# Grouped-query attention: GpSimd takes a fifth key tile in every fourth unit, and keys and an output half stand at other slots

## What is computed

```python
q = (query @ Wq + bq).reshape(B, L, NKV, G, HDIM)
k_, v_ = jnp.split(kv @ Wkv + bkv, 2, axis=-1)
...
scores = jnp.einsum('blkgd,bmkd->bkglm', q, k) * scale
attn = jax.nn.softmax(scores, axis=-1)
o = jnp.einsum('bkglm,bmkd->blkgd', attn, v).reshape(B, L, NHEAD * HDIM)
return o @ Wo + bo
...
x = x + jnp.tanh(g_xattn[0]) * _L0_xattn_ref(_layernorm(x, axis=-1), ctx_4096, ...)
x = x + jnp.tanh(g_ffn[0]) * _L0_ffn_ref(_layernorm(x, axis=-1), ...)
```

## Time and profile before

| | us |
|---|---|
| time, median of 3 runs | 2287.54 (2286.14 to 2289.63) |
| the profiled execution | 2287.23 |
| its span, first to last instruction | 2285.1 |
| TensorE busy | 2239.8 |
| VectorE busy | 1858.9 |
| ScalarE busy | 1667.6 |
| GpSimd busy | 1625.9 |

### The profile page before, as it was taken

How to read it: one execution, slowest core, us unless ns; L and a number is a source line. 1 busy time by engine, 2 the same in 40 slices (tenths; PEclk the granted TensorE clock), 3 DMA queues, 4 the chain that set the end, 5 groups by cost and what they waited for, 6 DMA issues and landing times.

```text
span 2285.1 us, 37480 instructions
## 1 busy us (share of the span) xinstructions
PE 2239.8 (98%) x12299; PEld 1929.9 (84%) x12299; DVE 1858.9 (81%) x3263; ACT 1667.6 (73%) x3184; POOL 1625.9 (71%) x1373
## 2 busy tenths in 40 slices
PE   7999999999999999999999999999999999999999
PEld 6888888888888888888888888888888888888875
DVE  5898888888888787887888788787787888788786
ACT  4777777777777777777777777777777777777773
POOL 5887887977658678757658778766757657667672
PEclk9999999999999999999999999999999999999999
DMA  7444343454233343326213333333423213223120
GB/s 262 142 151 140 127 156 129 159 193 164 93 112 113 110 157 94 129 88 206 93 54 135 113 132 121 113 128 110 169 88 100 93 63 108 68 91 100 56 102 37
DMA packets 140031, 273.97 MB, mean 120 GB/s; under 512 B 22048, under 2 KB 57408, under 8 KB 139584
## 3 DMA queue, kind: packets, MB, share of 16 engines
q1 hardware_dynamic: 124864, 257.85, 33.2%
q10 hardware_dynamic: 14976, 13.74, 2.6%
HBM read 202.44 MB, written 66.97 MB: 118 GB/s over the span
## 4 chain that ended last, share of the span: by engine, by line
PE 74%; DVE 14%; issue 5%; ACT 3%; POOL 3%; DMA 1%; ACTq 0%; DVEq 0%; SPq 0%; POOLq 0%
PE psW L454 11%; PE psW L456 11%; PE psW L455 11%; PE psS L454 6%; PE psS L456 6%; PE psS L455 6%; PE psW L684 6%; PE psW L687 5%; PE psW L686 5%; DVE psum_ L1442 4%; DVE mrun L1407 3%; PE psW L511 2%; DVE pl L1160 2%; POOL xs L898 1%; PE psW L519 1%
## 5 line engine op out<-in xcount | busy, mean ns | idle before, releaser
L898 POOL TENSOR_TENSOR xs<-xs,mb 128x512 f32<-128x512 f32 x832 | 1064.6, 1303 | 458.2 <-ACT mb L969 458.2
L1407 DVE TENSOR_TENSOR mrun<-psS,mrun 128x512 f32<-128x512 f32 (+1 forms) x704 | 481.6, 684 | 281.1 <-ACT xs L969 277.8
L969 ACT ACTIVATE xs<-psS 128x512 f32<-128x512 f32 x832 | 496.9, 597 | 224.6 <-PE psS L456 213.5
L1160 DVE TENSOR_TENSOR pl<-psP,ph 128x512 fp32r<-128x512 f32 (+1 forms) x672 | 458.6, 683 | 78.7 <-ACT ph L1102 74.7
L1102 ACT ACTIVATE ph<-xs 128x512 fp32r<-128x512 f32 x832 | 520.0, 625 | 3.0 <-PE psW L687 2.7
L1442 DVE TENSOR_TENSOR psum_<-psP,psum_ 128x512 f32<-128x512 f32 (+1 forms) x672 | 457.1, 680 | 2.0
L1099 ACT ACTIVATE psP<-xs 128x512 f32<-128x512 f32 (+1 forms) x672 | 402.4, 599 | 30.3 <-POOL xs L898 12.6
L454 PE MATMUL psS<-ql,kh 128*128 128x512 f32 x832 | 341.6, 411 | 7.1 <-DVE mrun L1407 6.1
L684 PE MATMUL psW<-ph,vh 128*128 128x512 f32 x832 | 334.9, 402 | 3.8 <-DVE pl L1160 1.6
L455 PE MATMUL psS<-qh,kh 128*128 128x512 f32 x832 | 327.5, 394 | 0.0
L456 PE MATMUL psS<-qh,kl 128*128 128x512 f32 x832 | 326.7, 393 | 0.0
(11 more groups left out here) (225 smaller groups left out, 4432.2 us busy)
## 6 DMA issues: line engine op xcount, KB each, us to landing
wqh<-scr_wq SPq DMA_DIRECT2D x96, 256.0 KB, 2.6
wql<-scr_wq SPq DMA_DIRECT2D x96, 256.0 KB, 3.0
woh<-scr_wo SPq DMA_DIRECT2D x47, 512.0 KB, 3.3
wol<-scr_wo SPq DMA_DIRECT2D x47, 512.0 KB, 4.2
rbc<-scr_r ACTq DMA_DIRECT2D x52, 256.0 KB, 3.4
scr_wq<-wqh SPq DMA_DIRECT2D x32, 256.0 KB, 2.2
scr_wq<-wql SPq DMA_DIRECT2D x32, 256.0 KB, 2.9
scr_wo<-woh SPq DMA_DIRECT2D x16, 512.0 KB, 2.7
```

The costliest lines, as they stand in the source:

```text
L898: eng.tensor_tensor(tile, tile, mb[:, U % 2, :], ALU.subtract).then_inc(s_sub)
L969: return eng.activation(hi, src, ACT.Copy)
L1160: return eng.tensor_tensor(lo, src, f32(hi), ALU.subtract)
L1407: eng.tensor_tensor(run, psS[0:rows, s % 2, :], a, ALU.max).then_inc(s_m)
```

## The change

Two things, in batches 1 to 3 the first, in all batches the second.

First, a function `by_pool(U)` says which tiles of a unit are GpSimd's. It is as before, save that in batches 1 to 3 units with U % 4 == 1 give it tile 4, the fifth, too. There are twelve (17, 21, ... 61); since tiles are worked on one unit later, the work lies in units 18, 22, ... 62, the third units of four. GpSimd makes the tile's lower part (L4) and adds the tile to the pair (A4); VectorE leaves both out. The full exponential of that tile goes to a third place of `pp`. The counts that the engines wait for (`ap_tile`, `ap_total`) follow.

Second, the last unit but one of a batch (14, 30, 46, 62) gets a string of its own: output half p0 stands in slot 1 instead of 4, the keys' last chunk k3 in slot 4 instead of 6.

```diff
--- before.py
+++ after.py
...
         return 1 if U < NU else 3
+    def by_pool(U):
+        return (0,) if U < NU else (0, 1, 2, 4) if U % 4 == 1 else (0, 1, 2)
     MEM_LO, MEM_SUM = 2, UN - 3
...
     ]
+    LAST_BUT_ONE = "m,v11 p0 b,v12 k2 k3 s - r,p1 q0 - q1 x0 o0,x1"
     TURN = "m,v11 p0 b,v12 k2 p1 s k3 r q0 - q1 - o0"
...
                     UN + 1: "- p1 c - s - o0 o1",
-                    UN - 1: "m - b - p1 s - r - - o0 - -"}.get(U, TURN if U > NU and U % NU == 2 else (AT_MEM if U >= MEM_LO + 2 else AT)[U % 4])
+                    UN - 1: "m - b - p1 s - r - - o0 - -"}.get(U, TURN if U > NU and U % NU == 2 else LAST_BUT_ONE if U % NU == NU - 2 else (AT_MEM if U >= MEM_LO + 2 else AT)[U % 4])
         for t, names in enumerate(names_of.split()):
...
         mrun = sb("mrun", [128, 2, 512], F32)
-        pp = sb("pp", [128, 2, 512], F32)
+        pp = sb("pp", [128, 3, 512], F32)
         mb = sb("mb", [128, 2, 512], F32)
...
             U, t = divmod(T, NT)
-            pool_tile = t < lead(U)
+            pool_tile = t in by_pool(U)
             for c, more in ((l_count, not pool_tile), (lp_count, pool_tile), (a_count, not pool_tile)):
...
                 in_psum.append(T)
+        ap_tile, ap_total, n = {}, {}, 0
+        for U in range(NU, UN):
+            if U > NU:
+                n += 1
+                ap_total[U - 1] = n
+            for a in by_pool(U)[2:]:
+                n += 1
+                ap_tile[U, a] = n
         def pair_of(U):
...
                 return psum_[:, U % 2, :]
-            if t < lead(U):
-                return pair_of(U)[:, t - 1, :]
+            if t in by_pool(U):
+                return pair_of(U)[:, by_pool(U).index(t) - 1, :]
             return psP[0:rows_of(t), (l_count[T] - 1) % 2, :]
...
                     else:
-                        pe.wait_ge(s_ap, 2 * (n - NU + 1))
+                        pe.wait_ge(s_ap, ap_total[n])
                     turn(("s", n, 0), psum_[:, n % 2, :], s_su, s_r, n + 1, sum_by_mem(n))
...
                     pe.wait_ge(s_vl, NT * (U // 4) + v_made(t))
-                    if t < lead(U):
+                    if t in by_pool(U):
                         pe.wait_ge(s_lp, lp_count[T])
...
             def add_p(T):
+                U, t = divmod(T, NT)
                 pool.wait_ge(s_lp, lp_count[T])
-                pair = pair_of(T // NT)
-                eng.tensor_tensor(pair[:, 0, :], pair[:, 0, :], pair[:, 1, :], ALU.add).then_inc(s_ap)
+                if t == 4:
+                    pool.wait_ge(s_ap, ap_tile[U, 2])
+                pair = pair_of(U)
+                eng.tensor_tensor(pair[:, 0, :], pair[:, 0, :], pair[:, by_pool(U).index(t) - 1, :], ALU.add).then_inc(s_ap)
             def merge(U):
...
                 pool.wait_ge(s_a, a_count[NT * U + NT - 1])
-                pool.wait_ge(s_ap, 2 * (U - NU) + 1)
+                pool.wait_ge(s_ap, ap_tile[U, by_pool(U)[-1]])
                 eng.tensor_tensor(total, pp[:, 0, :], total, ALU.add).then_inc(s_ap)
...
                 "S0,S1 M,S2 L0,S3 L1,S4 L2,S5 A2,S6 S7 S8 S9 S10 S11 S12 -",
-                "S0,S1 S2,S3 S4,L0 L1,L2 M,S5 S6,A2 S7 S8 S9 S10 S11 S12 -")]
+                "S0,S1 S2,S3 S4,L0 L1,L2 M,S5 S6,A2 S7 S8 S9 S10 S11 S12 -",
+                "S0,S1 M,S2 L0,S3 L1,S4 L2,S5 A2,S6 L4,S7 A4,S8 S9 S10 S11 S12 -")]
             for p in first:
...
                 if 0 <= U < UN:
-                    for step in steps_at[0 if lead(U) == 1 else 2 if U == UN - 1 else 1][t]:
+                    for step in steps_at[0 if lead(U) == 1 else 3 if 4 in by_pool(U) else 2 if U == UN - 1 else 1][t]:
                         if step == "M" and U > 0 and lead(U - 1) == 3:
...
                             act.wait_ge(s_su, U - 1)
-                    elif t < lead(U):
+                    elif t in by_pool(U):
                         if U == UN - 1:
...
                         elif U > NU:
-                            act.wait_ge(s_ap, 2 * (U - NU))
+                            act.wait_ge(s_ap, ap_total[U - 1])
                         else:
...
                 T = s - EXP
-                if 0 <= T < TN and T % NT >= lead(T // NT):
+                if 0 <= T < TN and T % NT not in by_pool(T // NT):
                     UT, tt = divmod(T, NT)
...
                         dve.wait_ge(s_a, a_count[T])
-                        dve.wait_ge(s_ap, 2 * (UT - NU) + 1)
+                        dve.wait_ge(s_ap, ap_tile[UT, 2])
                         eng.tensor_tensor(total, pair_of(UT)[:, 0, :], total, ALU.add).then_inc(s_a)
...
```

## The result

The changed kernel takes 2291.18 us (median of 14 runs, 2289.56 to 2294.8), the kernel before 2286.72 beside it (14 runs, 2284.76 to 2289.63): a ratio of 1.002, 95% interval 1.0014 to 1.0027, so 0.2% slower, about 4.5. The forecast was +1.4. The profiled execution took 2291.5 (2287.23 before), with a span of 2289.5 (2285.1) and a mean granted TensorE clock of 0.996 (0.999).

The account below looks back on a forecast made before the run. TensorE, busy 98% of the span, was taken to bound the kernel, so only its waits could shrink. Terms -3.2 - 0.2 + 6.2 - 1.4 = +1.4 on 2287.23 gave 2288.6, or 2288.9 as median; 8-in-10 range 2283.3 to 2292.8.

Parts of the forecast that it names:

- Part 1: Fifth tile on GpSimd, units 22, 26, 38, 42, 54, 58: scores wait less for running max, 0.53 each, -3.2.
- Units 18, 34 and 50: Fifth tile on GpSimd there: its work stays hidden with 0.1 to spare, nothing gained, 0.
- The slower rival: Fifth tile comes late at slot 10's product in every third unit; one more operation's lag gives 2297.5; chance 0.12.
- the third rival: VectorE's stalls vanish whole (6 x 0.78, unit 62 whole, unit 14 gains 1.2): 2285.4; chance 0.10.
- Unit 14: Keys and output half sooner, but the reciprocals' spread then waits for VectorE: -0.2, bounds -1.2 and +0.3.
- Units 30 and 46: GpSimd's fifth tile behind two normalisations: TensorE stands 4.2, unit 3.1 longer (bounds +2.4, +3.6), +6.2 for two.
- The faster rival: Normalisations don't hold the product in units 30 and 46, which gain 1.1 each: 2280.3; chance 0.12.
- Unit 62: Gains 1.1 in slot 7 and 1.2 from the fifth tile; slower second normalisation costs 0.9: -1.4, bounds -2.5, -0.7.
- The signs named in the prediction: Running-max waits 0.1 to 0.2, pl wait about 4 at slot 10 of units 30 and 46 alone, kl wait gone.
- part 2: Keys and an output half sooner in units 14, 30, 46, 62; 1.1 of unit 30's 1.33 wait gained.

Follow-up runs that it names:

- E2: Changed kernel without the fifth tile on GpSimd in any unit, only keys and output half moved sooner: 2282.78, ratio 0.9982 to the kernel before.
- E7: E4 with output half p1 also one slot sooner, in slot 6 of units 14, 30, 46 and 62: 2279.39, ratio 0.9968.
- E5: Changed kernel with 17 extra matmuls, unused in the result, filling TensorE's wait in slot 10 of units 30 and 46: 2288.3, ratio 1.0004.
- E4: Changed kernel with x normalisations of units 30 and 46 moved to slot 1, x loads to slot 6 of units 29 and 45: 2281.1, ratio 0.9976.
- E1: Changed kernel, but VectorE keeps the fifth tile in units 30 and 46: 2279.71, ratio 0.9969 to the kernel before.
- E6: Changed kernel with the second of two x normalisations moved behind GpSimd's fifth-tile lower half in units 30 and 46: 2286.64, ratio 0.9993.
- E8: E1 with output half p1 also in slot 6 of units 14, 30, 46 and 62: 2279.1, ratio 0.9964 to the kernel before.
- E3: Changed kernel with only the fifth tile on GpSimd, keys and output half standing as before: 2285.41, ratio 0.9996.
- E9: E7 with the loads of x issued in slot 10 of units 29 and 45 instead of slot 6: 2280.21, ratio 0.9966.

## Why the prediction was right or wrong

**Sign and size.** Forecast +1.4 with "no difference" as likeliest; measured +4.5, which lies at the bound of 0.2%, inside the range. The miss of 3.1 is nearly all in one term.

**Part 1, six units: right.** -3.2 forecast, -3.40 measured, -0.49 to -0.63 a unit. The scores of slot 12 start within 0.01 of the forecast time, because the price was read from ScalarE's chain (0.53) and not from VectorE's saving (1.20). E2, without part 1, has +0.12 there, so the gain is part 1's.

**Units 18, 34 and 50: right.** 0 forecast, +0.11 for the three, and a margin of 0.1 was enough: the product is at 667.68 in unit 18, with no wait. The slower rival, a fifth tile late in every third unit, doesn't occur. Nor does the third rival, by which VectorE's stalls vanish whole: it wanted 0.78 from each of the six units, and 0.49 to 0.63 came.

**Unit 14: right.** -0.2 forecast, -0.31 measured. As worked out, the spread of the reciprocals waits for VectorE, and takes most of the 1.1 back. TensorE in unit 14:

```profile
522.52 0.65 PE L536 MATMUL psW<-ident,rinv 128*128 128x128 f32 x4 [1.04 <-DVE rinv L1361]
522.93 0.48 PE L471 MATMUL psW<-wol,oh 128*128 128x512 f32 x1
```

E7, which puts work in front of this wait, gets 0.7 of it back in unit 14 and loses 0.2 to 0.3 in unit 15.

**Units 30 and 46: the mechanism right, the term mis-sized.** This is the step that failed. The prediction had GpSimd's chain at 7.50, 4.11 and 1.29; measured are 7.54 (1067.04 to 1074.58), 4.10 and 1.27. It had a stand of 4.2 and a unit 3.1 longer; E5 measures 3.14 and 3.09 for exactly that stand. What it left out is what TensorE does behind a stand. The term was +6.2 for the two units; it measured +9.69, and 3.5 of that is the work at half clock. The prediction counted a pause as lost time alone and took every matmul behind it at its old duration. Its own upper bound of +3.6 a unit was worked out from GpSimd's durations only, so neither +5.30 nor +4.39 lies within it.

In these units the kernel before could not show this: they hold no idle time over 1.1. Its start-up does. TensorE of the kernel before, timeline at the end of an idle time there, and the window behind it:

```profile
30.02 0.44 PE L454 MATMUL psW<-cl,wkh 128*128 128x384 f32 x1 [3.18 <-DVE cl L1160]
```

```profile
31.20:34.50 3.30, 3.30 (x11) 3.01 (x10) 0.48 (x1) 1.17 (x2) 0.20 (x1) 0.50 0.95 310
```

This pair was the row to ask for a price: an idle time of 3.18 with the clock at half for 3.41 behind it, that is some 1.7 of work lost, beside a forecast stand of 4.2 in each unit. With it the term would have been +3.1 + 1.7 twice, +9.6, against +9.69 measured. That this agrees so well is luck: the clock cost 2.2 in one unit and 1.3 in the other, because it stayed low for 5.1 and 3.0 behind the two products (1080.01 to 1085.07, 1631.62 to 1634.61), and how long that is the kernel before could not tell.

**The faster rival** (the normalisations don't hold the product) fell; E4 and E1 show that its price was right: with the hold taken away the units are 0.9 to 1.2 shorter (it said 1.1), and the whole is at 2281.1 and 2279.71 (it said 2280.3).

**Unit 62: right by half of its reason.** -1.4 forecast, -1.37 measured. VectorE in unit 62, the place of the earlier trace rows:

```profile
2177.34 0.54 DVE L1272 TENSOR_SCALAR hn<-x,mv,rstd 128x512 f32<-128x512 f32 x1
...
2181.38 1.68 DVE L1272 TENSOR_SCALAR xraw<-x,mv,rstd 128x512 f32<-128x512 f32 x1
2182.99 0.68 DVE L1428 TENSOR_TENSOR mrun<-psS,mrun 128x512 f32<-128x512 f32 x1
```

The second normalisation did lengthen as forecast, from 0.53 to 1.68 instead of 1.45. But the first, 1.45 before, is down to 0.54, and it wasn't touched. E6 has the same instructions in this unit, with 0.54 and 0.53, and the unit is -2.07 instead of -1.37. So the slow second one costs 0.7 of the 1.15 that it is longer, and whether it is slow isn't fixed by the program's order (the last section shows what goes with it). The term of -1.4 was hit with luck: of the five profiles with this string in unit 62 and both parts there, two more have -1.34 and -1.39 (E5, E4) and two -2.07 and -2.12 (E6, E1), and all of it lay in the bounds.

**The signs named in the prediction.** The six waits for the running max have shrunk so far that the list of waits leaves them out; the wait of 4 for `pl` at slot 10 of units 30 and 46 and the end of the waits for `kl` came as named. Unit 30 was to be "some 3 longer" and is 5.3 longer: this was the sign that told of the missing term.

## What to carry to other kernels

A stand of TensorE in a busy stretch can be dearer than its length: where the clock falls, add half of the work time at half clock (here 1.3 to 2.2 for stands of 1.9 to 4.0), and tell the two apart with a run in which the stand is filled by matmuls. Two edits that each gain may lose together where one makes an engine earlier, and perhaps delays another, and the second edit puts work on the engine that is then waited for: look at the places where the new orders meet, and leave one of the edits out there (E8) rather than both. When an engine's list gets a step, look at what else stands in the list in that slot only in some units; it is these units that decide the sign.

## What the runs showed of the hardware

**The clock falls behind short stands, and their length alone doesn't decide it.** Idle times of TensorE in units 30 and 46, and the clock behind them: 1.10 (E3), at 1.00 both times; 1.89 and 1.91 (E6), at half for 3.41 both times; 3.96 and 3.97 (changed kernel), at half for 6.83 and for 3.41. The stand filled with matmuls (E5): 1.00 both times. Three other places show how little the length says. In unit 63 all eleven kernels have the same idle time of 1.42 to 1.44 ahead of an output half; the clock fell behind it in E5 and E6 alone, for 3.41 each. TensorE there in the changed kernel and in E5:

```profile
2217.02 0.47 PE L471 MATMUL psW<-wol,oh 128*128 128x512 f32 x1 [1.42 <-issue]
```

```profile
2213.18 0.55 PE L473 MATMUL psW<-wol,oh 128*128 128x512 f32 x1 [1.42 <-issue]
```

That is unit 63's +2.25 in E5 and belongs to no edit. In unit 2 E8 falls to half behind an idle time of 1.67 (from 106.49, for 3.41), and the kernel before doesn't behind 1.75 at the same place:

```profile
106.01 0.68 PE L536 MATMUL psW<-ident,rinv 128*128 128x128 f32 x4 [1.67 <-DVE rinv L1361]
...
107.34 0.63 PE L473 MATMUL psS<-qh,kl 128*128 128x512 f32 x1
```

```profile
107.64 0.65 PE L519 MATMUL psW<-ident,rinv 128*128 128x128 f32 x4 [1.75 <-DVE rinv L1340]
...
108.36 0.40 PE L455 MATMUL psS<-qh,kh 128*128 128x512 f32 x1
```

And in the start-up the kernel before falls to half behind an idle time of 3.18 (from 31.17, for 3.41) while E7 and E8 don't behind 2.61 and 2.62 at the same place. What besides the length decides is open. The price in E6: its product starts 2.28 after its last matmul of scores (1076.10 to 1078.38), 2.05 more than at full pace (0.23), less the 1.17 that part 2 gains (E2): 0.9. The units are 2.5 longer, so 1.6 to 1.7 is the clock's.

**What varies from execution to execution of one kernel goes with its clock.** Of the executions of the kernel before beside E1 to E4, the 11 with a mean clock of 1.0 took 2284.84 to 2286.54, the 12 with 0.999 took 2286.58 to 2287.83, and the 4 with 0.997 or 0.998 took 2287.33 to 2289.73. So a profile without a fall in the start-up (E7: 2278.53, against a median of 2279.39) flatters its kernel, and one with several does the reverse (E4: 2282.91 against 2281.1).

**VectorE's normalisation (L1272 here, L1251 before, L1273 in E6; 128x512 from SBUF to SBUF) and GpSimd's operations take turns.** The two normalisations of unit 62 took 1.45 and 0.53 before, 0.54 and 1.68 after, 0.54 and 0.54 in E1, 0.79 and 0.70 in E3, 1.71 and 1.18 in E4, 0.54 and 0.53 in E6. The eleven profiles have 22 of them. One ran while GpSimd was idle and took 0.53. Eleven took 0.70 to 1.71, and each of these ended 0.28 or 0.29 after the end of an operation of GpSimd. Ten took 0.53 or 0.54 though GpSimd was busy; each began 0.1 to 0.2 ahead of an operation of GpSimd, which then took 1.49 to 1.59 instead of 1.29 or 1.30. The second normalisation's neighbour on GpSimd in the changed kernel, then the normalisation and its neighbour in E6:

```profile
2181.49 1.29 POOL L915 TENSOR_TENSOR xs<-xs,mb 128x512 f32<-128x512 f32 x1
```

```profile
2177.86 0.53 DVE L1273 TENSOR_SCALAR xraw<-x,mv,rstd 128x512 f32<-128x512 f32 x1
...
2177.96 1.58 POOL L915 TENSOR_TENSOR xs<-xs,mb 128x512 f32<-128x512 f32 x1
```

In both the normalisation begins 0.1 ahead of GpSimd's operation; in the changed kernel (2181.38 to 2183.06) it ends 0.28 behind the end of that operation, in E6 GpSimd's is the one that is longer. So which of the two pays is settled within a tenth of a microsecond, and an equal order gives both. The Trainium skill (GPSIMD Engine Reference, "Specifications") says that VectorE and GpSimd share SBUF interfaces and contend in some modes; these pairs agree, though no run took GpSimd's operation away at this place alone.

**A small store can be held up by large loads of another queue.** Two loads of 256 KB (a 128x512 tile of four-byte values each), issued 2.5 and 1.9 ahead of the store of the reciprocals (1032.56), made ScalarE wait 1.95 for it (E4) and 1.85 (E7); issued from 1041.24 on, behind the store, they left a wait of 0.5 (E9). The kernel before has no such loads there and goes from store to read-back in 3.14, E4 in 4.84.
